# Attention chain on one Trainium2 core: VectorE copies the upper rows of the turned maxima in two of the three attention stages

## The reference, cut to what matters

```python
# causal (layer 2)
scores = jnp.einsum('hbqd,hbkd->hbqk', Q_, K_) / d ** 0.5
scores = jnp.where(tril[None, None] == 0.0, NEG, scores)
attn = jax.nn.softmax(scores, axis=-1)
# banded (layer 3, self): mask = (j <= i) & (i - j < 64), bias by head and distance
# full   (layer 3, cross): no mask, no bias
a = jax.nn.softmax(s, axis=-1)
o = jnp.einsum('bhqk,bhkd->bhqd', a, v)
```

## Time and profile before

| | |
|---|---|
| runs, median of 3 | 1765.01 us (1758.82 to 1767.97) |
| profiled execution | 1767.88 us, span 1766.1 us |
| TensorE busy | 1555.6 us, 88% of the span |
| VectorE busy | 902.9 us, 51% |
| ScalarE busy | 739.4 us, 42% |
| chain that ended last | PE 61%, issue 15%, DVE 11%, ACT 5% |
| mean granted TensorE clock | 0.936 of full speed |

### The profile page before, as it was taken

One profiled execution on the slowest core, in us unless ns is written; L12 is line 12 of the kernel. 1 busy time (PEld: TensorE's weight loads), 2 busy tenths in 40 slices (PEclk: granted clock), 3 DMA queues, 4 the chain that ended last, 5 costly groups with the idle time before them and its releaser, 6 DMA issues.

```text
span 1766.1 us, 26713 instructions
## 1 busy us (share of the span) xinstructions
PE 1555.6 (88%) x9276; PEld 815.9 (46%) x9308; DVE 902.9 (51%) x2236; ACT 739.4 (42%) x1289; POOL 251.0 (14%) x116
## 2 busy tenths in 40 slices
PE   5999898888999988878999998887899998889786
PEld 2337455434434645632533554563253355465234
DVE  2662665482465365557156437455625635645661
ACT  0761344264265243517236325252724631624352
POOL 1003111201101112110110201211011031112102
PEclk9998898989999889889999979998999997989899
DMA  9002104503100211250310030224111003031300
GB/s 336 1 7 36 37 1 73 108 1 114 50 1 7 36 37 24 50 108 1 113 50 1 7 58 15 50 60 72 43 72 49 1 14 65 2 68 43 59 25 12
DMA packets 44867, 84.13 MB, mean 48 GB/s; under 512 B 10416, under 2 KB 28592, under 8 KB 44464
## 3 DMA queue, kind: packets, MB, share of 16 engines
q1 hardware_dynamic: 39680, 68.98, 15.4%
q10 hardware_dynamic: 5040, 13.28, 3.7%
HBM read 42.37 MB, written 2.10 MB: 25 GB/s over the span
## 4 chain that ended last, share of the span: by engine, by line
PE 61%; issue 15%; DVE 11%; ACT 5%; DMA 3%; ACTq 2%; POOL 2%; DVEq 0%; POOLq 0%
PE ring L1135 7%; PE obank L1145 7%; PE ring L1125 7%; DVE nmax L955 6%; PE ring L1086 5%; PE ring L1378 4%; PE obank L1340 4%; PE ring L1321 3%; PE ring L1201 3%; PE ring L1304 3%; PE ring L1290 3%; PE ring L1107 2%; ACT region_e L709 2%; PE ring L1073 2%; DMA q_all<-q_parts 2%
## 5 line engine op out<-in xcount | busy, mean ns | idle before, releaser
L955 DVE TENSOR_REDUCE nmax<-ring 128x2 f32<-128x1024 f32 (+4 forms) x384 | 318.6, 855 | 175.7 <-PE ring L1290 120.9
L709 ACT ACTIVATE region_e<-ring 128x1024 f32<-128x1024 f32 (+4 forms) x384 | 269.8, 733 | 115.6 <-PE ring L1290 81.2
L819 DVE CUSTOM_DVE_ANT_0 region_d<-ring,maskb 128x512 f32<-128x512 f32 x256 | 165.8, 686 | 101.1 <-issue 101.1
L606 ACT ACTIVATE region_e<-region_d,nmin 128x512 f32<-128x512 f32 x256 | 182.6, 714 | 81.7 <-DVE nmin L819 80.1
L701 ACT ACTIVATE q_all<-ring 2x1024 fp32r<-2x1024 bf16 x96 | 97.6, 1016 | 230.1 <-DVE nmax L955 116.3
L1290 PE MATMUL ring<-cbf 64*128 64x128 bf16 (+1 forms) x2048 | 169.7, 251 | 0.0
L1304 PE MATMUL ring<-k_tiles_a,q_all 64*128 64x512 f32 (+4 forms) x384 | 98.3, 514 | 47.8 <-DMA q_all<-q_parts 40.7
L1135 PE MATMUL ring<-region_q 64*128 64x512 f32 x512 | 126.1, 613 | 5.4 <-ACT region_q L595 5.4
L539 POOL TENSOR_TENSOR nat_x<-nat_n,rows 128x1024 f32<-128x1024 f32 x16 | 37.7, 2354 | 649.9 <-DVE nat_n L864 486.4
L1145 PE MATMUL obank<-region_e,vs 128*64 128x512 f32 x512 | 124.0, 605 | 0.0
L1321 PE MATMUL ring<-q_all,k_tiles_a 64*128 64x512 f32 (+4 forms) x384 | 91.9, 470 | 22.9 <-ACT q_all L701 12.4
(11 more groups left out here) (171 smaller groups left out, 2226.3 us busy)
## 6 DMA issues: line engine op xcount, KB each, us to landing
k_tiles_a<-k_parts SPq DMA_DIRECT2D x144, 64.0 KB, 2.3
k_tiles_b<-k_parts SPq DMA_DIRECT2D x144, 64.0 KB, 2.3
q_all<-q_parts ACTq DMA_DIRECT2D x144, 64.0 KB, 3.4
q_all<-q_parts SPq DMA_DIRECT2D x144, 64.0 KB, 3.2
region_b<-in_w_f SPq DMA_DIRECT2D x8, 1024.0 KB, 5.1
wvo<-in_wv SPq DMA_DIRECT2D x4, 1024.0 KB, 8.2
wqk<-in_wq SPq DMA_DIRECT2D x4, 1024.0 KB, 10.1
wqk<-in_wk SPq DMA_DIRECT2D x4, 1024.0 KB, 12.1
```

The costliest lines, as they stand in the source:

```text
L606: ins = act.activation(e0[:, n % E0, h, :], sm0[:, n % 2, h, :], ACT.Exp, bias=nmin0[:, n, h:h + 1], scale=-1.0, accum_out=sum0[:, n, h:h ...
L709: act.activation(e16[:, n % 4, 2 * u:2 * u + 2, 0:nq], slot((a, "B", g, kt, u))[:, :, 0:nq], ACT.Exp)\
L819: ins = dve.tensor_tensor_reduce(out=sm0[:, n % 2, h, :], in0=slot(("S0", p, kt))[:, h, :], in1=maskb[:, :], scale=-1.0, scalar=3.0e38, op ...
L955: dve.tensor_reduce(nmax[:, qt, 2 * u:2 * u + 2], slot(name)[:, :, 0:nk], AX.X, ALU.max, negate=True)\
```

## The change

In the causal and the banded stage ScalarE copies only the rows on partitions 32 and 33. The rows on 96 and 97 are copied by VectorE, in a new step `far_rows` that stands straight behind `maxima_cols` in VectorE's program. It signals a new semaphore, `rows_turned`. TensorE waits for it in two places: before the first B piece of a group, and before a job that takes over the slot of such a T. In the full stage nothing changes.

```diff
-                    for at in (32, 96):
+                    for at in (32, 96) if a == FULL else (32,):
                         ins = act.activation(q_tiles[g][at:at + 2, :, :], turned[at:at + 2, :, :], ACT.Copy)
                     ins.then_inc(*ends_drain((a, "T", g)))
...
+                def far_rows(a, g):
+
+                    dve.wait_ge(*filled_by((a, "T", g), b))
+                    dve.wait_ge(q_stacked[g], (b * 3 + a + 1) * 96)
+                    turned = slot((a, "T", g))[:, 0, :].bitcast(BF16).rearrange("p (u q) -> p u q", u=2)
+                    dve.tensor_copy(q_tiles[g][96:98, :, :], turned[96:98, :, :]).then_inc(rows_turned, 1)
...
                     maxima_cols(a, 0)
+                    if a != FULL:
+                        far_rows(a, 0)
...
                             if kind == "M":
                                 maxima_cols(a, *which)
+                                if a != FULL:
+                                    far_rows(a, *which)
                             if kind == "H":
                                 head_out(a, *which)
...
                     pe.wait_ge(*free_for(name, b))
+                    before = JOBS[JOB[name] - SLOTS]
+                    if len(before) > 2 and before[1] == "T" and before[0] != FULL:
+                        pe.wait_ge(rows_turned, b * 2 * GROUPS + before[0] * GROUPS + before[2] + 1)
...
                     if (kt, u) == (0, 0):
                         pe.wait_ge(*drained_by((a, "T", g), b))
+                        if a != FULL:
+                            pe.wait_ge(rows_turned, b * 2 * GROUPS + a * GROUPS + g + 1)
```

More of the change, by code:

```diff
@@ L313, in build @@
         mcol_ready = sem("mcol_ready")
+        rows_turned = sem("rows_turned")
         heads_ready = sem("heads_ready")
```

## The result

| | before | after |
|---|---|---|
| runs, median | 1765.95 us (4 runs, 1758.82 to 1767.97) | 1785.80 us (4 runs, 1777.69 to 1789.36) |
| profiled execution | 1767.88 us, span 1766.1 | 1784.02 us, span 1782.2 |
| mean granted TensorE clock, profiled | 0.936 | 0.925 |

The ratio of the runs is 1.0113, with a 95% interval of 1.0067 to 1.0159. The changed kernel is slower by 19.85 us on the medians. The forecast was 10.3 us more, 1775.5 us, with a range of 1763 to 1786. The sign is right and the time lies inside the stated range, at its very upper end. The amount is off by nearly a factor of two, and it lies above the band of +4.7 to +16 us that the prediction gave its own forecast: the stated range reaches it only because it was stretched to rival 3.

A forecast was written before the change was run, and what follows sets the result against it. TensorE, busy 88% of the span, was taken as the bound, so other engines count only where it waits. 8 x (1.8 - 0.54 - 0.87 + 0.5 + 0.4) = +10.3 us gave 1775.5 us, range 1763 to 1786.

The forecast's parts named there:

- rival 3: Long clock falls behind the third T (1.4 us), A pieces slowed at the first (+0.86): +21 us, 1786; chance 0.16.
- The copy's length: VectorE's new copy of 1024 elements from PSUM takes 1.22 us, like its nearest PSUM read of 1.221 us.
- rival 1: VectorE's copy is quick, 0.61 us: -4.4 us with no clock fall, 1761, within 0.5%; chance 0.12.
- Third T, the shift of H: VectorE's output step H starts later behind the copy, delaying maxima and the B piece: +1.8 us at 8 places.
- Rival 2: VectorE and TensorE catch up the late H between third and fourth T: -9.7 us, 1755; chance 0.08.
- The clock behind the third T: TensorE's new 2.5 us stand brings a short clock fall at somewhat more than half of 8 places: +0.4 us each.
- Second T: No H there; maxima of the A piece and then the B piece start earlier: -0.54 us at 8 places.
- Fourth T: B piece in T's slot and ScalarE's exponentials start earlier: -0.87 us at 8 places.
- First T: Maxima of two A pieces wait behind VectorE's copy, ScalarE's saving is lost: +0.5 us at 8 places.

The follow-up runs named there:

- experiment 3: Changed kernel plus 8 idle matmuls on TensorE in its stand behind the third T; 1776.36 us, ratio 1.0045 to the kernel before.
- Experiment 7: Kernel before plus six idle matmuls on TensorE ahead of the first B piece at the first T, causal and banded; 1760.12 us, ratio 0.9953.
- experiment 5: Against the kernel before, VectorE copies the upper rows only at the first T of the causal and banded stage; 1775.32 us, ratio 1.0037.
- experiment 2: Against the kernel before, VectorE copies the upper rows only at the second and fourth T, causal and banded; 1743.39 us, ratio 0.9857.
- experiment 4: Kernel before, no VectorE copy, but at the third T, causal and banded, VectorE waits for T to be filled before H; 1781.79 us, ratio 1.0079.
- experiment 6: Against the kernel before, VectorE copies the upper rows only at the fourth T of the causal and banded stage; 1756.98 us, ratio 0.9932.
- experiment 8: Against the kernel before, VectorE copies at the second and fourth T only, plus six idle matmuls at the first T; 1743.49 us, ratio 0.9849.
- experiment 1: Against the kernel before, VectorE copies the upper rows only at the third T of the causal and banded stage; 1797.34 us, ratio 1.0176.

## Why the prediction was right in sign and short in size

- **The copy's length**: 1.22 us taken, 1.230 measured. The quick copy (rival 1) is out.
- **Third T, the shift of H**: +1.8 us a place predicted, 1.86 and 1.88 measured in experiment 3, where the clock stays up. The step was right: the copy waits for T, H waits for the copy, the maxima wait for H, and TensorE waits for the maxima, 2.65 us where 2.5 was forecast. Rival 2, that the late H is made up before the fourth T, is out.
- **The clock behind the third T**: +0.4 us a place predicted, from a short fall at somewhat more than half of the places. This is the term that was mis-sized. It fell at 8 of 8 places and cost 14.6 us, 1.8 us each. Both factors were too low. The price was read from the step from first to second T, as the 0.69 us between a fall of 7 us and one of 3.5. Experiment 7, without a fall there, gives the price at that place outright: 0.9 us for the short one and 1.6 for the long one. Behind the third T the same lengths cost more: the causal places with a fall of 7 us are 2.1 and 2.3 us longer than the shift explains (15.54 and 15.83 us against 11.63 + 1.86), those with a fall of 3 to 4 us 1.4 (14.94 and 14.91). So a price from one stretch did not hold in another; why a fall costs less behind the first T is not shown. With 1.8 in place of 0.4 the sum would be 8 x (1.8 - 0.54 - 0.87 + 0.5 + 1.8) = 21.5 us, against 19.85 measured. The four measured steps add up to 19.9 us, but that they meet the runs so closely is in part luck: the whole profiled execution is only 16.1 us longer, since untouched stretches were 3.8 us shorter.
- **Second T**: -0.54 a place predicted, 4.3 us; -4.1 measured.
- **Fourth T**: -0.87 a place, 7.0 us; -7.6 measured up to the next stage.
- **First T**: +0.5 a place, 4 us; +2.1 in the profile after, +2.9 in experiment 5. Here the spread is one of where the clock falls: in the profile after, TensorE stands for 1.94 us at all 8 places, and two banded stages have no fall and are 0.47 us shorter than before.
- **Rival 3**, the clock going further, with 16% and +21 us, came closest to what happened. It had the long fall at 1.4 us and the dearer first T; the first T stayed cheap, and the fall behind the third cost more. So its 1786 us, hit to the microsecond, comes of two errors that nearly cancel.
- **The range**: its lower end was said to be rival 1, but rival 1 gives 1761 us, not 1763.

What stays open: in experiments 2, 4, 6 and 8 the runs moved by 4 to 10 us more than the steps that the edit touches. Experiment 2 shows it most, with 10.6 us in the full stage and the other layers; in experiments 4 and 6 it is hardly clear of the noise. In the profile before, each of the four passes has one fall of about 17 us that begins in layer 1; in that of experiment 2 each of these falls is of 7 us. This is not a mark of the edit alone: of the same four falls two are of 7 us in the changed kernel's profile, three in that of experiment 1 and one in that of experiment 3. The windows of 1 us in the second pass, of before and then of experiment 2:

```profile
595.00:596.00 1.00, 1.00 (x4) 0.67 (x2) 0.74 (x2) 0.22 (x1) 0.00 (x0) 0.50 0.64 111
...
610.00:611.00 1.00, 1.00 (x4) 0.30 (x2) 0.96 (x7) 0.00 (x0) 0.00 (x0) 0.50 0.03 8
```

```profile
595.00:596.00 1.00, 1.00 (x6) 1.00 (x7) 0.00 (x0) 0.00 (x0) 0.00 (x0) 0.50 0.44 82
...
602.00:603.00 1.00, 0.56 (x2) 0.30 (x2) 1.00 (x6) 1.00 (x2) 0.00 (x0) 1.00 0.00 0
```

The two profiles are not at the same place of the program at 595. In before the fall begins with the matmuls of the second `gate` job, 199.2 us after the fourth T of the full stage. In experiment 2 those run at full pace, and the fall begins 205.6 us after that T, in the later `cnt` job. The first four matmuls of the second `gate` job in both, before first:

```profile
594.56 2.00 PE L1219 MATMUL ring<-w_gt,region_q 128*128 128x256 f32 x4
```

```profile
587.94 1.13 PE L1235 MATMUL ring<-w_gt,region_q 128*128 128x256 f32 x4
```

It also ends earlier, at 601 instead of 612. A later fall of 3 to 7 us follows in both. Ahead of this fall of before TensorE had no stand of over 0.2 us for 13 us; the last was one of 0.84 us, up to 581. I did not test what decides between the two.

## What to carry to other kernels

Before work is put on the engine that is less busy, look at what stands behind it in that engine's queue. Here VectorE was busy for only 51%, but a copy that waits for TensorE, placed ahead of a 2.6 us output step, cost more than it saved on ScalarE. The same copy at the second and fourth T, where no piece that TensorE needs waits behind an output step, won 13 us in its own steps, 0.7%; the kernel's runs gained 1.4%, and the rest is not explained. The copy at the third T placed behind H was not tried. And price a new stand of TensorE twice: its length, and a fall of the clock behind it. Take the price of the fall from the stretch in question: here it was 0.9 to 1.6 us behind the first T and 1.2 to 2.5 us behind the third.

## What the hardware did that was not expected

- A stand of TensorE of 2.5 to 2.7 us behind the third T was followed by the lower clock at 8 of 8 places in the changed kernel, costing 1.2 to 2.5 us each, and at 8 of 8 in experiment 1.
- The length of a short stand alone did not decide. Stands of 0.82 and 0.59 us, close together, were followed by a fall at three of four places in experiment 4. A stand of 0.52 us (causal) or 0.82 us (banded) behind the third T was followed by none in the 8 places of before, but by one at two of the 8 places in experiment 5, and at one of 8 each in experiments 7 and 8, though no edit touches that place. The 17 us fall in layer 1 of before, in the second pass, had no stand of over 0.2 us in the 13 us ahead of it.
- Eight bf16 matmuls of 128x512 whose result nothing reads (seven in the record, 1.67 us) in a stand of 2.65 us kept the clock at 1.00 behind the third T and brought the changed kernel from 1.0113 to 1.0045 of the kernel before, some 12 us; the two intervals just meet, at 1.0067.
- The falls of the clock in untouched stages differ from kernel to kernel: two kernels that differ from before only at the fourth or at the first T have steps elsewhere in the causal and banded stages that are up to 1.5 us longer or shorter, and full stages and layers up to 3 us. That the timing change moves them is likely but not shown apart from chance, with one profile of each.
